# Edge counting of a graph layer moved into the attention stages, in groups of 16 nodes instead of 32

## The chip, the cores and the metric

The kernel runs on one core of a Trainium2 chip. The time is that of the device, in microseconds (us). The engines are TensorE (PE, with its weight loads as PEld), VectorE (DVE), ScalarE (ACT), GpSimd (POOL) and SyncE (SP); here SP only issues transfers. Each engine is fed by its own sequencer, which also executes register operations and branches; the trace shows those under the engine's name with a q (PEq, PEldq, DVEq).

## The reference, cut to what matters

One block of a graph transformer over N = 1250 nodes of 768 values. `_gat_layer` is run twice (4 heads of 512, then 1 head of 768).

```python
xn = layernorm(x)
# GAT layer: edges (src, dst), 41250 of them sorted by dst, and one loop per node added
h = xn @ W;  al_s, al_d = h . a_src, h . a_dst
e = leaky_relu(al_s[src] + al_d[dst], 0.2)
m = segment_max(e, dst);  ex = exp(e - m[dst])
alpha = ex / (segment_sum(ex, dst)[dst] + 1e-16)
out = segment_sum(h[src] * alpha, dst) + bias
# mix: linear attention with random features, 8 heads of 96
q, k, v = (xn @ qkv_w.T + qkv_b), q and k scaled
phi = exp(q @ rf.T - |q|^2/2);  kv = phi_k.T @ v
attn = phi_q @ kv / (phi_q @ sum(phi_k));  mix = attn @ proj_w.T + proj_b
x = x + gat2(elu(gat1(xn))) + mix
x = x + experts(layernorm(x))      # 32 experts, 2 groups x 2 experts per token
```

## The kernel before

The stages run one after another, each in its own block; at the end of a block all engines meet, and all stages keep to this order: `norm_phase`, `mix_half_phase` and `numerator` for half 0 (4 heads), the same for half 1, `proj_phase`, `logits` with `edge_table`, `count_phase`, `mask_phase`, `gat1_phase`, `gat2_project_phase`, `gat2_phase`, routing and experts. Inside a block each engine runs its own list in the order in which it is written; semaphores join them. Nodes are worked on in NT = 10 tiles of P = 125.

**The graph as counts.** The kernel never gathers along edges. It builds the dense matrix c[dst, src] of edge multiplicities and works with masks and weighted sums over it. `edge_table` loads src and dst as 324 rows of 128 edges, splits each source into a part `hi` and a rest `slo` below SLO = 314 (SPLIT = 4 parts), and forms the key dst·4 + hi. Transposed on PE they are `keyT` and `sloT`. Since dst is sorted, a group of WIN = 32 nodes touches a short span of rows; DVE and a PARTITION_ALL_REDUCE on POOL find the NW = 40 spans, in steps of RB = 4 rows.

**`count_phase`** (profile lines L779 on) works through the 40 groups, 4 heads by 10 tiles, one group beside one gemm. PE: a 12-matmul gemm for h of that head and tile (L863), a matmul that opens the PSUM sum `count_S` (L867), then a loop over the span's steps, each with 4 matmuls (L872) of a one-hot [128 edges x 128 keys] with a one-hot [128 edges x 314 sources], and one that closes the sum (L878). DVE makes both one-hots of a step (L842 one instruction, L848 four) into a ring of 4 steps ahead of PE. The bounds of the loop are read from the table at run time (value loads, L809 and L810), the branch is L814, and the ring's slot is worked out in registers. For the edges of these inputs there are 120 steps, 3 in most groups. ACT moves h and the counts out; SP stores the counts.

**`mask_phase`** loads the counts back with a node's four parts side by side, adds the loops (L974), makes the mask (ACT, L1008), finds the maxima m (DVE, L987) and transposes the count tiles (PE, L1024).

**A mix half** does one tile at a time (`tile`): transposes of q (L590), gemm q of the next tile (L580), transposes of k, gemm k, the two pairs of feature matmuls (L598), gemm v, and the 16 halves of `keys_values` (L608). DVE adds biases and norms, ACT squares, copies and takes exponentials, POOL copies the next tile of xnT into `mix_xs`. The first gemm waits for the weights and for `mix_rfT`.

**`gat2_project_phase`** goes twice through the ten tiles of h1 (q = 0 to 19). SP loads each (L1275) when the product before last is done, along with weights and masks, and at q = 12 all of x1 (`x<-x_dram`), with the residual, for the next stage.

Of the kernel before, what the change touches and what calls it, by code (L numbers as in the profile page):

```python
# [7 lines left out]
F16 = mybir.dt.float16  # L8
# [20 lines left out]
RB = 4  # L29
# [3 lines left out]
WIN = 32  # L33
NW = 40
SPLIT = 4
SLO = 314
# [85 lines left out]
def norm_phase(nc, cx, x, ident, xnT, load_next):  # L122
# [4 lines left out]
        ("stats_done", "sqrt_done", "xn_ready", "transposed", "used_dve", "used_act", "id_done"))  # L127
    dve_step = cx.sem("norm_dve_step")
    HT = NT // 2
    with ExitStack() as st:  # L130
# [7 lines left out]
        xn = [sb(nc, st, f"xn{b}", [P, D]) for b in range(2)]  # L138
        tp = [[pb(nc, st, f"tp{b}{h}", [128, 3, P]) for h in range(2)] for b in range(2)]
        block = st.enter_context(nc.Block())  # L140

        @block.sync
        def _(sp):
            for h in range(2):
                rows_dma(sp, xa[:, h * HT:(h + 1) * HT, :],
                         x.rearrange("(t p) d -> p t d", p=P)[:, h * HT:(h + 1) * HT, :], x_loaded[h])
            load_next(sp)

        @block.gpsimd
        def _(pool):  # L150
            pool.memset(ident[:], 0.0).then_inc(id_done, 1)
            pool.wait_ge(id_done, 1)
            pool.affine_select(out=ident[:], in_=ident[:], compare_op=ALU.not_equal, fill=1.0, base=0,
                               pattern=[[-1, 128]], channel_multiplier=1).then_inc(id_done, 1)

        @block.vector
        def _(dve):
            step = Chain(dve, dve_step)
            for t in range(NT):
# [12 lines left out]
            def scaled(t, b):  # L172
                dve.wait_ge(transposed, t + 1)
                dve.tensor_scalar(xn[b][:], xa[:, bass.ds(t, 1), :], mv[:, bass.ds(t, 1), 0],
                                  rstd[:, bass.ds(t, 1)], ALU.subtract, ALU.mult).then_inc(xn_ready, 1)

            def copy(t, b):
                dve.wait_ge(transposed, t + 3)
                dve.tensor_copy(xnT[:, 0:3, bass.ds(t * P, P)], tp[b][0][:]).then_inc(used_dve, 1)

            scaled(0, 0)
            with dve.Fori(0, NT // 2 - 1) as i:
                for b in range(2):
                    scaled(i * 2 + (b + 1), 1 - b)
                    copy(i * 2 + b, b)
            scaled(NT - 1, 1)
            copy(NT - 2, 0)
            copy(NT - 1, 1)

        @block.scalar  # L190
        def _(act):
            act.wait_ge(stats_done, 1)
            act.activation(std[:], veps[:], ACT.Sqrt).then_inc(sqrt_done, 1)
            with act.Fori(0, NT // 2) as i:
                for b in range(2):
                    act.wait_ge(transposed, i * 2 + (b + 3))
                    act.activation(xnT[:, 3:6, bass.ds(i * (2 * P) + b * P, P)], tp[b][1][:],
                                   ACT.Copy).then_inc(used_act, 1)

        @block.tensor  # L200
        def _(pe):
            pe.sem_inc(transposed, 2)
            pe.sem_inc(used_dve, 2)
            pe.sem_inc(used_act, 2)
            pe.wait_ge(id_done, 2)
            with pe.Fori(0, NT // 2) as i:
                for b in range(2):
                    pe.wait_ge(xn_ready, i * 2 + (b + 1))
                    pe.wait_ge(used_dve, i * 2 + (b + 1))
                    pe.wait_ge(used_act, i * 2 + (b + 1))  # L210
                    for k in range(KD):
                        last = pe.transpose(tp[b][k // 3][:, k % 3, :], xn[b][:, k * 128:(k + 1) * 128],
                                            ident[0:P, 0:P])
                    last.then_inc(transposed, 1)

# [226 lines left out]
def load_mix_weights(sp, half, wqkvT, qkv_b, w, brow, w_loaded):  # L442

    HW = D // 2
    for c in range(3):
        cols = slice(c * D + half * HW, c * D + (half + 1) * HW)
        sp.dma_start(w[:, :, c, :], wqkvT[:, cols].rearrange("(k p) n -> p k n", p=128)).then_inc(w_loaded, 16)
        sp.dma_start(brow[:, c, :], qkv_b[cols].partition_broadcast(128)).then_inc(w_loaded, 16)


def mix_half_phase(nc, cx, half, rfT_dram, xnT, ident, w, brow, w_loaded, attn, gnn_w1, a_src, a_dst, wa, load_next):


# [4 lines left out]
    SCALE = MD ** -0.5  # L458
    tag = f"mix{half}_"
    (rf_loaded, staged, q_done, k_done, v_done, q_evac, k_evac, v_evac, qsq, ksq, q_ready, k_ready, q_turned,  # L460
     k_turned, qT_done, kT_done, phi_a, phi_b, exp_a, exp_b, kv_step, kv_copied, consts) = (
        cx.sem(tag + s) for s in
        ("rf_loaded", "staged", "q_done", "k_done", "v_done", "q_evac", "k_evac", "v_evac", "qsq", "ksq", "q_ready",
         "k_ready", "q_turned", "k_turned", "qT_done", "kT_done", "phi_a", "phi_b", "exp_a", "exp_b", "kv_step",
         "kv_copied", "consts"))
# [3 lines left out]
    with ExitStack() as st:  # L469
        rfT = sb(nc, st, tag + "rfT", [A, RF])  # L470
# [1717 lines left out]
```

## Time and profile before

| what | value |
|---|---|
| median of 3 runs | 2376.53 us (2363.14 to 2378.86) |
| the profiled execution | 2375.32 us, span in the trace 2373.5 us |
| PE busy | 2108.3 us, 89% |
| DVE busy | 1124.8 us, 47% |
| ACT busy | 413.1 us, 17% |
| POOL busy | 202.7 us, 9% |

The span is what lies between the first and last record of the trace; 1.8 us lie around it. [...] Stages in the trace, by their first record: norm 0 to 42.6, mix half 0 to 212.9 with its numerator to 257.1, half 1 to 431.5 and 473, projection to 581.8, logits and edge table to 604.1, counting to 901.9, masks to 985.8, GAT 1 to 1365, then the rest.

### The profile page before, as it was taken

How to read it: one execution, taken by the hardware profiler on the slowest of the kernel's cores; microseconds unless marked ns; L12 is line 12 of the kernel's file. 1: busy time of each engine (PE TensorE's matmuls, PEld its weight loads, DVE VectorE, ACT ScalarE, POOL GpSimd, SP SyncE). 2: the span in 40 equal slices, each digit the busy share in tenths (PEclk: the TensorE clock that was granted, in tenths of full speed). 3: DMA queues.
4: the chain of work that ended last, by engine and by line, in shares of the span. 5: the costliest groups of instructions: out<-in, count | busy, mean ns of one | idle time of the engine just before them, and what ended most of it. 6: DMA issues, size and time to landing. Idle time of an engine off the chain costs nothing. (4 is left out here: it accounts for less than half of the span.)

```text
span 2373.5 us, 33698 instructions
## 1 busy us (share of the span) xinstructions
PE 2108.3 (89%) x9786; PEld 1471.1 (62%) x9787; DVE 1124.8 (47%) x2406; ACT 413.1 (17%) x743; POOL 202.7 (9%) x198
## 2 busy tenths in 40 slices
PE   4998999879799994299999979898986799999997
PEld 2666666644355553288888845454564577777776
DVE  4114211436566665788888700206636333333433
ACT  1222121200111113222222200001100122122221
POOL 0000000000000001000000000000001133323332
PEclk9999999889899995599999989998975799999999
DMA  7002200172200007633433265622125488898654
GB/s 224 0 0 70 90 0 0 43 221 71 92 25 22 24 22 246 212 96 116 121 97 98 73 220 180 168 85 75 42 59 216 123 243 258 253 285 283 187 140 78
DMA packets 79502, 288.38 MB, mean 121 GB/s; under 512 B 10780, under 2 KB 31328, under 8 KB 69837
## 3 DMA queue, kind: packets, MB, share of 16 engines
q1 hardware_dynamic: 57894, 220.18, 28.0%
q0 software_dynamic: 14688, 54.19, 9.7%
q10 hardware_dynamic: 6854, 13.15, 1.6%
q8 instruction: 40, 0.66, 0.1%
q14 instruction: 26, 0.21, 0.0%
HBM read 225.48 MB, written 62.00 MB: 121 GB/s over the span
## 5 line engine op out<-in xcount | busy, mean ns | idle before, releaser
L1215 PE MATMUL gat_Z<-h,gat_wt 125*125 125x256 f32 (+1 forms) x1600 | 355.0, 381 | 20.7 <-DVE gat_wt L1131 20.7
L1215 PEld LDWEIGHTS gat_Z<-h,gat_wt 125*125 125x125 f32 x1600 | 298.2, 188 | 66.1 <-DVE gat_wt L1131 21.2
L580 PE MATMUL mix_G<-mix_w,mix_xs 128*125 128x384 f32 x720 | 242.6, 488 | 0.0
L1363 PE MATMUL gat2p_Y<-gat2p_w,gat2p_hT 128*125 128x386 f32 (+1 forms) x640 | 211.8, 493 | 19.8 <-DMA gat2p_w<-in_L_gnn_W 10.4
L863 PE MATMUL count_G<-gnn_w,xnT 128*125 (+1 forms) x480 | 214.1, 596 | 15.3 <-issue 15.3
L2033 PE MATMUL ex_PH<-ex_xT,ex_w 128*128 128x128 f32 x1872 | 223.5, 278 | 3.0 <-issue 1.0
L2043 PE MATMUL ex_PY<-ex_w,ex_hT 128*128 128x384 f32 x624 | 215.1, 495 | 3.3 <-ACT ex_hT L1982 2.8
L2033 PEld LDWEIGHTS ex_PH<-ex_xT,ex_w 128*128 128x128 f32 x1872 | 214.3, 193 | 4.8 <-issue 4.4
L1363 PEld LDWEIGHTS gat2p_Y<-gat2p_w,gat2p_hT 128*125 128x125 f32 x640 | 121.0, 190 | 109.2 <-issue 14.2
L580 PEld LDWEIGHTS mix_G<-mix_w,mix_xs 128*125 128x125 f32 x720 | 133.1, 189 | 84.9 <-issue 2.2
L2043 PEld LDWEIGHTS ex_PY<-ex_w,ex_hT 128*128 128x128 f32 x624 | 114.3, 190 | 80.3 <-ACT ex_hT L1982 5.9
L863 PEld LDWEIGHTS count_G<-gnn_w,xnT 128*125 128x125 f32 x480 | 88.4, 189 | 114.7 <-issue 113.2
L1477 PE MATMUL gat_Z<-h,gat_wt 125*125 125x385 f32 (+1 forms) x400 | 132.4, 494 | 11.0 <-DVE gat_wt L1435 11.0
L842 DVE SCALAR_TENSOR_TENSOR count_A<-count_ikey,count_off,keyT 128x512 f32 x120 | 90.2, 751 | 96.6 <-issue 63.9
L533 DVE TENSOR_REDUCE mix_nrm<-mix_sq 125x4 f32<-125x384 f32 x40 | 22.1, 553 | 215.5 <-ACT mix_sq L553 215.5
L1477 PEld LDWEIGHTS gat_Z<-h,gat_wt 125*125 125x125 f32 x400 | 76.0, 190 | 67.4 <-DVE gat_wt L1435 11.6
L848 DVE TENSOR_SCALAR count_B<-count_islo,sloT 128x314 f16 x480 | 112.1, 298 | 0.0
L1953 DVE TENSOR_SCALAR ex_idS<-ex_ids 128x1 int32 x52 | 8.0, 154 | 214.5 <-DMA out_rows<-ex_y,ex_idS 214.5
L1923 DVE SCALAR_TENSOR_TENSOR ex_Q<-posm,offs,ex_iota 125x1280 bf16<-125x1280 f32 x55 | 85.3, 1552 | 42.7 <-issue 38.5
L1904 POOL DMA_INDIRECT out_rows<-ex_y,ex_idS x52 | 82.5, 1586 | 267.6 <-DVE ex_y L1955 223.1
L370 PE MATMUL proj_Y<-proj_w,proj_aT 128*125 128x384 f32 x240 | 83.1, 506 | 12.5 <-DVE proj_x L410 12.5
L1990 ACT ACTIVATE ex_y<-ex_PY,ex_gate 128x384 f32<-128x384 f32 x52 | 30.2, 580 | 280.6 <-DMA out_rows<-ex_y,ex_idS 242.9
(293 smaller groups left out, 2343.8 us busy)
## 6 DMA issues: line engine op xcount, KB each, us to landing
ex_w<-in_L_ffn_W SPq DMA_DIRECT2D x64, 1152.0 KB, 8.6
gat_cnt<-c_dram SPq DMA_DIRECT2D x50, 546.9 KB
gat2p_hT<-h1T_dram SPq DMA_DIRECT2D x20, 1000.0 KB, 5.0
h1T_dram<-gat_oT ACTq DMA_DIRECT2D x40, 250.0 KB, 2.0
mix_w<-in_L_mix_qkv_w SPq DMA_DIRECT2D x6, 1152.0 KB, 11.8
ct_dram<-count_out SPq DMA_DIRECT2D x40, 157.0 KB, 2.1
mix_w_slice<-in_L_gnn_W SPq DMA_DIRECT2D x6, 1024.0 KB, 11.5
proj_w2s<-in_L_gnn_W SPq DMA_DIRECT2D x4, 1536.0 KB, 26.1
```

The source lines that it names most:

```text
L370: last = pe.matmul(Y[j][:], aT[b][:, k, :], w[:, k, j * 384:(j + 1) * 384], start=(k == 0), stop=(k == KD - 1))
L580: last = pe.matmul(G[c][:], xs[b][:, k, :], w[:, k, c, :], start=(k == 0), stop=(k == KD - 1))
L842: dve.scalar_tensor_tensor(A[:, bass.ds(s * RB, RB), :], ikey[:].unsqueeze(1).to_broadcast([128, RB, 128]), off[:, bass.ds(hd * NT + t, 1) ...
L848: last = dve.tensor_scalar(B[:, bass.ds(s * RB + b, 1), :], islo[:].unsqueeze(1), sloT[:, bass.ds(r * RB + b, 1)], None, ALU.is_equal)
L863: last = pe.matmul(G[t % 2][:], xnT[:, k, t * P:(t + 1) * P], w[:, k, bass.ds(hd * C1, C1)], start=(k == 0), stop=(k == KD - 1))
L1215: last = pe.matmul(Z[b][j][:], wt[b][:, s, :], h[:, s, bass.ds(hd, 1), j * HC:(j + 1) * HC + j], start=(s == 0), stop=(s == NT - 1))
L1363: last = pe.matmul(Y[b][j][:, 0:HW if j else W], hT[q % 2][:, k, :], w[:, k, cols], start=(k == 0), stop=(k == KF - 1))
L1477: last = pe.matmul(Z[b][j][:], wt[b][:, s, :], h2[:, s, 385 * j:385 * j + CW[j]], start=(s == 0), stop=(s == NT - 1))
L1904: pool.indirect_dma_start(out, bass.IndirectOffsetOnAxis(ap=idS[:, 0:1], axis=0), y[:], None, compute_op=ALU.add).then_inc(added, 16)
L1923: dve.scalar_tensor_tensor(Q[:], posm[:, :, bass.ds(e, 1)].to_broadcast([P, NT, SLOT]), offs[:, bass.ds(at, 1)], iot[:].unsqueeze(1).to_br ...
L2033: last = pe.matmul(PH[m][:], w1[:, b, k, m * 128:(m + 1) * 128], xT[:, k, :], start=(k == 0), stop=(k == KD - 1))
L2043: last = pe.matmul(PY[j][:], hT[:, k, :], w2[:, b, k, j * 384:(j + 1) * 384], start=(k == 0), stop=(k == KM - 1))
```

## The change

- **The edge table** is made in `norm_phase`, on DVE before the statistics of x. SP loads the edges; ACT issues the loads of x, of rfT (once, kept for both halves) and of the mix weights.
- **Counting** is done in the mix halves, 40 groups in each, four a tile: one after gemm q, one after gemm k, one between the two feature pairs, one between gemm v and `keys_values`. There are now NW = 80 groups of WIN = 16 nodes, SPLIT = 8 parts of 157 sources, and steps of RB = 2 rows in a ring of 8. For these inputs they are 241 steps, 3 in most groups. The features share one PSUM bank, the counts have one. Tile loops of the norm and mix stages are written out. POOL no longer copies `mix_xs`; gemms read xnT.
- **`first_layer_phase`** takes the place of `logits`, `count_phase` and `mask_phase`: logits, then 40 gemm units for h; from unit 3 on, after every second unit the ten transposes of one count tile; after unit 30 those of m. DVE and ACT make masks beside it, now stored as BF16. The head's weights come in two buffers. A `cx.clear()` (semaphores set back) is added ahead of it.
- **The projection's weights** are loaded into the space of the mix weights.
- **`gat2_project_phase`** loads x1 in ten pieces, one each from q = 10 on.

```diff
-RB = 4
+RB = 2
-WIN = 32
-NW = 40
-SPLIT = 4
-SLO = 314
+WIN = 16
+NW = 80
+SPLIT = 8
+SLO = 157
...
 def norm_phase(...)
         @block.vector
         def _(dve):
             step = Chain(dve, dve_step)
+            dve.wait_ge(loaded, 8 * 16)
+            step(dve.tensor_copy(df[:], di[:]))
+            step(dve.tensor_copy(sf[:], si[:]))
+            step(dve.tensor_scalar(hi[:], sf[:], float(SLO), None, ALU.is_ge))
+            for part in range(2, SPLIT):
+                step(dve.scalar_tensor_tensor(hi[:], sf[:], float(part * SLO), hi[:], ALU.is_ge, ALU.add))
...
 def mix_half_phase(...)
+                    def window(i):
+                        win = half * PER * NT + i
+                        lo, hi = span(dve, win)
+                        with dve.Fori(lo, hi) as r:
+                            n = dve.snap(turn)
+                            s = dve.snap(n & (RING - 1), min_val=0, max_val=RING - 1)
+                            dve.wait_ge(used, n)
+                            dve.scalar_tensor_tensor(CA[:, bass.ds(s * RB, RB), :],
...
+                            for b in range(RB):
+                                last = dve.tensor_scalar(CB[:, bass.ds(s * RB + b, 1), :], islo[:].unsqueeze(1),
...
+                            last.then_inc(hot, 1)
+                            dve.reg_add(turn, turn, 1)
...
+                    def window(i, lo, hi):
+                        if i >= 1:
+                            pe.wait_ge(s_evac, i)
+                        pe.matmul(S[:], czero[:], islo[:], start=True, stop=False, skip_group_check=True)
+                        with pe.Fori(lo, hi) as _:
+                            n = pe.snap(count)
+                            s = pe.snap(n & (RING - 1), min_val=0, max_val=RING - 1)
+                            pe.wait_ge(hot, n)
+                            for b in range(RB):
+                                last = pe.matmul(S[:], CA[:, bass.ds(s * RB + b, 1), :].rearrange("p o k -> p (o k)"),
...
+                            last.then_inc(used, 1)
+                            pe.reg_add(count, count, 1)
+                        pe.matmul(S[:], czero[:], islo[:], start=False, stop=True, skip_group_check=True
+                                  ).then_inc(counted, 1)
...
+                    for t in range(NT):
+                        more = t + 1 < NT
+                        turn(0, t)
+                        if more:
+                            gemm(0, t + 1, q_done, q_evac)
+                        window(PER * t, *span(pe, half * PER * NT + PER * t))
+                        turn(1, t)
+                        if more:
+                            gemm(1, t + 1, k_done, k_evac)
+                        window(PER * t + 1, *span(pe, half * PER * NT + PER * t + 1))
+                        features(t, 0)
+                        window(PER * t + 2, *span(pe, half * PER * NT + PER * t + 2))
+                        features(t, 1)
+                        if more:
+                            gemm(2, t + 1, v_done, v_evac)
+                        window(PER * t + 3, *span(pe, half * PER * NT + PER * t + 3))
+                        keys_values(t, not more)
...
 def first_layer_phase(...)
+            for g in range(1, UNITS):
+                unit(g)
+                t = (g - MASK0) // 2
+                if g >= MASK0 and (g - MASK0) % 2 == 0 and t < NT:
+                    pe.wait_ge(looped, t + 1)
...
+                    for s in range(NT):
+                        last = pe.transpose(T[t % 2][s // 4][0:P, s % 4 * P:(s % 4 + 1) * P],
+                                            ct[t % 2][:, s * P:(s + 1) * P], ident[0:P, 0:P])
...
 def gat2_project_phase(...)
-                elif q - 2 == NT:
-                    rows_dma(sp, x1, x1_dram.rearrange("(t p) d -> p t d", p=P), x_loaded)
+                if q >= NT:
+                    rows_dma(sp, x1[:, q - NT, :], x1_dram[(q - NT) * P:(q - NT + 1) * P, :], x_loaded)
```

How it moves instructions. PE in a mix tile, before: transposes of k, gemm k, both feature pairs, gemm v and `keys_values` stand in one row of matmuls (the same names as in the trace; the brackets name the semaphores).

```order
L590 MATMUL mix_TQ<-ident,mix_qs 97x125 [waits mix0_qT_done,mix0_k_ready]
L590 MATMUL mix_TQ<-ident,mix_qs 97x125 x3
L580 MATMUL mix_G<-mix_w,mix_xs 125x384 [waits mix0_k_evac]
L580 MATMUL mix_G<-mix_w,mix_xs 125x384 x5
L598 MATMUL mix_PH<-mix_rfT,mix_kT 125x256 [waits mix0_exp_a,mix0_kT_done]
L598 MATMUL mix_PH<-mix_rfT,mix_kT 125x256
L598 MATMUL mix_PH<-mix_rfT,mix_kT 125x256 [waits mix0_exp_b]
L598 MATMUL mix_PH<-mix_rfT,mix_kT 125x256
```

The same place after, from the loop of the third group of a tile to the second feature pair (REGISTER_ALU, ISA and the branch are the sequencer's).

```order
L753 REGISTER_ALU [waits mix0_count_hot]
L753 ISA
L753 REGISTER_ALU
L753 MATMUL mix_count_S<-mix_count_B,mix_count_A 128x157
L753 ISA
L753 REGISTER_ALU
L753 MATMUL mix_count_S<-mix_count_B,mix_count_A 128x157
L757 ISA
L748 COMPARE_AND_BRANCH
L758 MATMUL mix_count_S<-mix_count_islo,mix_count_zero 128x157
L723 MATMUL mix_PH<-mix_rfT,mix_kT 125x256 [waits mix0_k_exped,mix0_kT_done]
L723 MATMUL mix_PH<-mix_rfT,mix_kT 125x256
```

A loop with two matmuls a step, whose wait stands on a register operation, now lies between the feature pairs, and three more like it elsewhere in the tile.

DVE at the start of the norm stage, before: the statistics come first.

```order
L163 BN_STATS stats<-xa 125x6 [waits norm_x_loaded0]
L163 BN_STATS stats<-xa 125x6 x9
L163 BN_STATS stats<-xa 125x6 [waits norm_x_loaded1]
L163 BN_STATS stats<-xa 125x6 x9
L166 BN_AGGR mv<-stats 125x2 [waits norm_dve_step]
L166 BN_AGGR mv<-stats 125x2 x9
```

And after, from the start of the table.

```order
L194 CAST edge_df<-edge_di 108x384 [waits edge_loaded]
L195 CAST edge_sf<-edge_si 108x384 [waits norm_dve_step]
L196 TENSOR_SCALAR edge_hi<-edge_sf 108x384 [waits norm_dve_step]
L198 SCALAR_TENSOR_TENSOR edge_hi<-edge_sf,edge_hi 108x384 [waits norm_dve_step] x6
L199 SCALAR_TENSOR_TENSOR edge_slo<-edge_hi,edge_sf 108x384 [waits norm_dve_step]
L200 SCALAR_TENSOR_TENSOR edge_key<-edge_df,edge_hi 108x384 [waits norm_dve_step]
L201 TENSOR_REDUCE edge_rng<-edge_df 108x3
```

The whole table, with its wait for the edges, stands ahead of the statistics of x.

## Rows read from the trace of the kernel before

**Rows 1.** The page: busy time, share and instructions of each engine.
```profile
PE 2108.3 (89%) x9786; PEld 1471.1 (62%) x9787; DVE 1124.8 (47%) x2406; ACT 413.1 (17%) x743; POOL 202.7 (9%) x198
```

**Rows 2.** Windows: us; busy PE, PEld, DVE, ACT, POOL; clock, DMA share, GB/s.
```profile
42.60:212.90 170.30, 163.59 (x684) 110.16 (x684) 31.35 (x74) 45.88 (x70) 8.57 (x12) 0.99 0.08 32
...
581.80:604.10 22.30, 17.39 (x52) 5.19 (x52) 9.91 (x32) 1.76 (x4) 1.62 (x5) 0.81 0.29 89
604.10:901.90 297.80, 283.42 (x1040) 143.05 (x1040) 190.84 (x600) 41.21 (x80) 0.98 (x6) 0.98 0.10 38
901.90:985.80 83.90, 26.87 (x110) 22.88 (x110) 62.46 (x95) 26.76 (x40) 10.90 (x21) 0.50 0.79 255
```

**Rows 3.** Timeline of PE, a mix tile: start, duration, group, [idle before].
```profile
75.25 0.59 PE L590 MATMUL mix_TQ<-ident,mix_qs 125*97 125x125 f32 x4
75.68 4.04 PE L580 MATMUL mix_G<-mix_w,mix_xs 128*125 128x384 f32 x12
...
89.46 1.92 PE L608 MATMUL mix_KV<-mix_vs,mix_phik 125*128 125x97 f32 x16
91.22 0.59 PE L590 MATMUL mix_TQ<-ident,mix_qs 125*97 125x125 f32 x4
```

**Rows 4.** Timeline of PE in counting: a gemm and what follows it.
```profile
623.70 5.31 PE L863 MATMUL count_G<-gnn_w,xnT 128*125 128x512 f32 x12
628.85 0.30 PE L867 MATMUL count_S<-count_islo,count_zero 128*128 128x314 f16 x1
```

**Rows 5.** PE's sequencer by line: duration ns, first and last start (us).
```profile
L809 PEldq TENSOR_LOAD <-spans x1: 313/313/313, 621.7 to 621.7; - x1
L814 PEldq MOVE  x1: 29/29/29, 623.1 to 623.1; - x1
L815 PEldq MOVE  x3: 29/29/29, 742.8 to 745.9; - x3
L872 PEldq FUSED_REGOPS  x4: 74/74/79, 743.0 to 743.7; - x4
L632 PEldq COMPARE_BRANCH  x1: 207/207/207, 88.9 to 88.9; - x1
```

**Rows 6.** Timeline of DVE: start of the norm stage, start of the edge table.
```profile
12.15 4.70 DVE L163 BATCH_NORM_STATS2 stats<-xa 125x6 f32<-125x384 f32 x10 [12.02 <-DMA xa<-in_x]
...
591.87 0.36 DVE L733 CAST edge_df<-edge_di 108x384 f32<-108x384 int32 x1 [10.33 <-DMA edge_si<-in_src]
...
593.06 1.15 DVE L737 SCALAR_TENSOR_TENSOR edge_hi<-edge_sf,edge_hi 108x384 f32<-108x384 f32 x2
```

**Rows 7.** Timeline of PE and POOL: first gemm of mix 0, start of counting.
```profile
47.36 12.10 PE L580 MATMUL mix_G<-mix_w,mix_xs 128*125 128x384 f32 x36
...
612.46 0.24 POOL L830 IOTA count_ikey<- 128x128 f32 x1 [11.17 <-issue]
...
615.16 6.82 PE L863 MATMUL count_G<-gnn_w,xnT 128*125 128x512 f32 x12 [15.31 <-issue]
```

**Rows 8.** Timeline of DVE in counting: two steps, then the next group's first.
```profile
617.09 0.75 DVE L842 SCALAR_TENSOR_TENSOR count_A<-count_ikey,count_off,keyT 128x512 f32 x1
...
618.65 0.75 DVE L842 SCALAR_TENSOR_TENSOR count_A<-count_ikey,count_off,keyT 128x512 f32 x1
...
621.43 0.75 DVE L842 SCALAR_TENSOR_TENSOR count_A<-count_ikey,count_off,keyT 128x512 f32 x1 [1.17 <-issue]
```

**Rows 9.** Timeline of PE: matmuls after gaps of some 2 us, and without.
```profile
205.53 0.67 PE L590 MATMUL mix_TQ<-ident,mix_qs 125*97 125x125 f32 x4 [1.97 <-DVE mix_qs L534]
...
213.48 10.36 PE L247 MATMUL mix_F<-mix_qT,mix_rfT 97*128 x24 [1.90 <-ACTq L264]
...
420.11 1.15 PE L590 MATMUL mix_TQ<-ident,mix_qs 125*97 125x125 f32 x4 [1.97 <-DVE mix_qs L534]
...
454.20 8.59 PE L247 MATMUL mix_F<-mix_qT,mix_rfT 97*128 x24
```

**Rows 10.** Timeline of PE in `gat2_project_phase`.
```profile
1529.18 33.00 PE L1363 MATMUL gat2p_Y<-gat2p_w,gat2p_hT 128*125 128x384 f32 x96 [9.42 <-DMA gat2p_hT<-h1T_dram]
```

More of the change, by code:

```diff
@@ L181, in _, with scaled @@
[L181 to L188, printed above, removed]
+            def scaled(t):
+                if t >= 2:
+                    dve.wait_ge(transposed, t - 1)
+                dve.tensor_scalar(xn[t % 2][:], xa[:, t, :], mv[:, t, 0:1], rstd[:, t:t + 1], ALU.subtract, ALU.mult
+                                  ).then_inc(xn_ready, 1)
@@ L200, in _ @@
         @block.tensor
         def _(pe):
-            pe.sem_inc(transposed, 2)
-            pe.sem_inc(used_dve, 2)
-            pe.sem_inc(used_act, 2)
             pe.wait_ge(id_done, 2)
[L206 to L214, printed above, removed]
+            pe.wait_ge(key_ready, 1)
@@ L475, in mix_half_phase @@
         with ExitStack() as st1:
-            xs = [sb(nc, st1, tag + f"xs{b}", [128, KD, P]) for b in range(2)]
             qs = sb(nc, st1, tag + "qs", [P, 2, HH, A])
@@ L574, in gemm @@
-                def gemm(c, t, b, done, evac):
-                    if c == 0:
-                        pe.wait_ge(staged, t + 1)
-                    if evac is not None:
+                pe.sem_inc(used, RING)
+                def gemm(c, t, done, evac):
+                    if t == 0:
+                        pe.wait_ge(w_loaded[c], 16 * (half + 1))
+                    else:
                         pe.wait_ge(evac, t)
                     for k in range(KD):
-                        last = pe.matmul(G[c][:], xs[b][:, k, :], w[:, k, c, :], start=(k == 0), stop=(k == KD - 1))
+                        last = pe.matmul(G[c][:], xnT[:, k, t * P:(t + 1) * P], w[:, k, c, :], start=(k == 0),
+                                         stop=(k == KD - 1))
@@ L976, in _ @@
             loop(0)
+            loop(1)
+            dve.wait_ge(al_turned, 1)
+            step(dve.tensor_copy(al[:], T[1][0][0:P, 0:NT * J].rearrange("p (t j) -> p t j", j=J)))
             dve.wait_ge(rows_loaded, 64)
@@ L1026, in _, with unit @@
-            pe.wait_ge(copied, NT)
-            pe.wait_ge(m_ready, 1)
-            for j in range(3):
-                for t in range(width[j]):
-                    last = pe.transpose(T[0][j][0:H1, t, :], m[:, 4 * j + t, :], ident[0:P, 0:P])
-                last.then_inc(m_turned, 1)
+            def unit(g):
+                hd, t = g // NT, g % NT
+                if t == 0:
+                    pe.wait_ge(w_loaded[hd % 2], 16 * (hd // 2 + 1))
+                if g >= 2:
+                    pe.wait_ge(h_evac, g - 1)
+                for k in range(KD):
+                    last = pe.matmul(G[g % 2][:], xnT[:, k, t * P:(t + 1) * P], w[hd % 2][:, k, :],
+                                     start=(k == 0), stop=(k == KD - 1))
+                last.then_inc(gemm, 1)
@@ new lines, in _ @@
+            for c in range(CH):
+                for k in range(KD):
+                    last = pe.matmul(T[0][c][0:J, 0:CHW[c]], wa[:, k, :], xnT[:, k, CHO[c]:CHO[c] + CHW[c]],
+                                     start=(k == 0), stop=(k == KD - 1))
+                last.then_inc(rows_done, 1)
+            unit(0)
+            pe.wait_ge(rows_copied, CH)
+            for t in range(NT):
+                last = pe.transpose(T[1][0][0:P, t * J:(t + 1) * J], alT[:, t * P:(t + 1) * P], ident[0:J, 0:J])
```

720 lines of the change are left out of this document (320 added, 400 removed).

## The prediction

> **What bounds the kernel now.** I read the page's busy shares first: PE is busy 89% of the span, DVE 47%, and nothing else comes near [rows 1]. So the question for every stage is whether PE is packed there, and I read the stages one by one in the view of windows [rows 2]. In the mix half PE is busy 163.59 of 170.30 us, in counting 283.42 of 297.80. The stage after counting is different: in the 83.9 us of the mask stage PE works 26.87 us at a granted clock of 0.50, DVE 62.46. Then the timeline of PE, for what a packed stage consists of. A mix tile runs from 75.25 to 91.22, 15.96 us, with no idle time in its rows: a transposition group of 0.43, a 12-matmul gemm of 3.9, and 1.8 for KV [rows 3]. A group of counting begins with one gemm of 5.15 us (623.70 to 628.85), and its count matmuls follow without a gap [rows 4]. Last the sequencer's own records, which the page does not count as busy [rows 5]: they are what the moved work is made of.
>
> **What goes.** From the end of the projection stage to the start of the first GAT block, 581.80 to 985.80 (its last 0.1 included), the kernel spends 404.1 us. After the change one block stands there: logits and their transposes (16.7 of the 17.39 us in [rows 2]; six edge transposes leave), 40 gemm units of 5.15 = 206.0, 100 count transposes and 10 of m. In the mask stage 110 transposes took 26.87 us at half clock, 0.24 each; at full clock, between gemms, I take half, so 13.2. With 0.9 for the last evacuation, 1.4 for the end of the block and 1.0 for the clearing that is added: 239.2. That is **−165**. DVE's 62.5 us and ACT's 26.8 of mask work lie beside it: a mask tile has two units and ten transposes, 11.5 us, for 6.2 of DVE, so they cost nothing; were one mask tile late each time, the stage would be bound by DVE at 62, still under the gemms. Bounds: −155 (transposes at half clock) to −170.
>
> **Edge table in the norm stage.** DVE begins its statistics at 12.15, after waiting for x [rows 6]. Now it first does the table. In its own stage DVE was busy 9.91 us [rows 2], almost all with the table; about 1.2 of it comes after the reduction. Four more comparisons (1.15 for two, [rows 6]) and tables twice as wide bring the rest to 11.7. The edges landed 9.3 us into the old block (581.8 plus a wait that ends at 591.87, [rows 6]), and now share the queues with x, so DVE starts on them at 9 to 15, ends at 21 to 27, and then has 9.4 of statistics (4.70 a half) that before began at 12.15 and could run only as x came in; they end 5 to 12 later; the tail (final operations on the spans, two copies) adds 2.2. Together **+10**, from +5 to +14.
>
> **Starts of the mix halves.** After PARTITION_ALL_REDUCE POOL's next operation came 11.17 us later with nothing waited for but "issue", and PE's first gemm of counting stood at 615.16, 11.1 us into its block; in mix half 0 it stood at 47.36, 4.8 in [rows 7]. The change puts the reduction and then IOTA in that order around the start of mix half 0, whose gemm now waits for the constants. Between 0 and +6.3; the row with the same order of operations is the nearest, so **+5.5**. Half 1 has no reduction before it and no load of rfT: **−1**. The last stores of counts at each end: **+1**.
>
> **Counting in the mix tiles.** It costs PE little and its sequencer much. The array: count matmuls of 157 columns cost about what KV's of 97 do, 0.11 (1.8 for 16, [rows 3]), so a window with 6 of them and its two borders is 0.8, four in a tile 3.2. The sequencer: two loads of a span and what follows take 1.4 (621.7 to 623.1); an iteration took 1.56 for 4 matmuls (three starts between 742.8 and 745.9); and one matmul's register work 0.245 (four between 743.0 and 743.7) [rows 5]. With 2 matmuls an iteration is then 1.56 − 0.49 = 1.07, and a window of three steps 1.4 + 3.2 = 4.6. Before, 1.4 + 3 × 1.56 = 6.1 of this in a group lay beside 7.1 of array work (283.42 / 40). Now, for 15.96 + 3.2 us of array work, there are 4 × 4.6 = 18.4 of sequencer work, and what decides is how far the sequencer may be ahead. It executed the tile's loop branch at 88.9, when KV, which stands ahead of that branch, began at 89.46 [rows 3, 5]: it was some 17 matmuls ahead and no further. So a window is hidden only behind what directly precedes it:
> - KV, turn 0 and gemm q run 6.1 us on the array; window 0 is hidden and adds 0.7;
> - turn 1 and gemm k (4.3) stand beside issuing them and window 1's 4.6 of sequencer work: 4.7 until its end;
> - window 2 has only two feature matmuls ahead: 4.7, almost all of it idle array;
> - the second features and gemm v (4.7) hide window 3, which adds 0.8: 5.5.
>
> The period is 21.7, with 0.2 for semaphores 21.9: **+5.9 a tile**. The first tile of a half has +5.5, eight have 47.2, and the last, where windows follow one another with no gemm between, +11.3. A half is +64 and both **+128**. Bounds: 3.2 a tile (all hidden), which makes +80, and 18.4 a tile beyond the array (nothing hidden), which is excluded by the first bullet.
>
> **DVE in the tile.** An iteration took it 1.56 (617.09 to 618.65) and a new span 1.17 more [rows 8]. Its work halves, to 0.8; its register work does not quite. I take 1.1, as on PE: 4 × (1.17 + 3.3) + 2.9 of its other work = 20.8, under 21.9, so it costs nothing, but only just. ACT's copies of the counts (four of 0.4) are beside.
>
> **The clock.** Window 2 leaves the array nearly idle for 3.4 us in each tile. Gaps of 1.9 to 2.0 us were followed by half clock in two places: the transposes at 420.11 took 1.15 where those at 205.53, after an equal gap, took 0.67; and the 24 matmuls after a gap of 1.90 at 213.48 took 10.36 against 8.59 without one at 454.20 [rows 9]. So a gap costs 0 to 1.8. I take 1.45 for 18 tiles and 2 for the ends: **+28**, bounds 0 and 36.
>
> **gat2_project.** PE waits 9.42 us at 1529.18 for hT [rows 10], whose load stands on SP's queue behind the one load of all of x (3.84 MB). In ten pieces, each issued after an hT, it holds none up. **−11**, with 1.6 for slower matmuls after the gap, an estimate by the pair at 213.48 and 454.20 [rows 9]; what is next late is nothing I see, since the weights' and masks' loads stay where they are. At least −5.
>
> **Sum.** +10 + 5.5 − 1 + 1 + 128 + 28 − 165 − 11 = −4.5. The profiled execution took 2375.3 (span 2373.5), 1.2 under the median of 2376.5. So 2370.8, rounded to **2370**: a large gain behind and nearly as large a loss ahead of it. About 1% (24 us) is what a measurement of this kernel can tell from no change.
>
> [...]
>
> **Rivals.**
> - **A, the clock holds.** The sparse matmuls of window 2 count as work, as after the gap at 205.53. 2370 − 28 = 2342. For: 205.53; against: 213.48 and 420.11.
> - **B, the sequencer's work is hidden.** Then a tile is 15.96 + 3.2 = 19.2, a half 9 × 3.2 + 11 = 40 instead of 64, and nothing lets the clock fall: 2370 − 48 − 28 = 2294. Against: the lead of 17 matmuls, and that windows 1 to 3 need 4.6 each with 0.8, 4.3 and 4.7 beside them.
> - **C, slower: DVE sets the tile.** PE's step waits for DVE's count masks in its sequencer, so everything behind it waits, the next gemm too. The point is (21.9 − 2.9)/4 − 1.17 over 3 = 1.19 us an iteration. At 1.4 the period is 24.4, +2.5 × 20 = +50: 2420; at the old 1.56 it is 26.4, 2460. For: DVE's reads of registers, its wait and its branch do not shrink with the tile; against: half its array work goes.
>
> **Chances.** The forecast 0.40, A 0.25, B 0.11, C 0.24. The range takes in A with the bounds of the small terms, and C up to 1.4 us an iteration: 2325 to 2418; B and the far end of C stay out. Faster by over 1% are A and B: 0.36; slower by over 1% is C: 0.24; the rest 0.40.
>
> **What would show it.** In the new profile: tiles of the mix halves of 21 to 23 us, with PE idle under "issue" in the third window and granted clock under 1 behind it; a first-layer block of about 239 with PE packed; the norm stage some 10 longer; POOL's IOTA late in mix half 0; no wait of PE for hT in gat2_project. I would be wrong by a period of 19 or of 25, and PE's waits in its sequencer for DVE's steps would show the latter.

## The result, and the profile after

The changed kernel takes **2417.2 us** (median of 4, 2414.9 to 2419.3); the kernel before took 2369.8 in the runs beside it (4, 2361.1 to 2378.9). The ratio is 1.020, interval 1.015 to 1.025: **slower by 2%**, where 2370 was forecast. The time is at the top of the range (2325 to 2418), the direction is that of rival C. The kernel before has times in two groups, 2361 to 2363 and 2376.5 to 2379 here, for which the last section has a likely stage; its profiled execution is of the upper one. The profiled executions took 2375.3 and 2416.7 us; their traces span 2373.5 and 2414.9 from the first record to the last, 1.8 less each, and differ by 41.4. I account for those.

By stage, from the first record of one to that of the next:

| stage | before | after | change | forecast |
|---|---|---|---|---|
| norm | 42.6 | 68.4 | +25.8 | +10 |
| mix half 0 | 170.4 | 276.0 | +105.6 | +83 |
| mix half 1 | 174.4 | 261.2 | +86.8 | +78 |
| first layer (logits, counting, masks before) | 404.1 | 236.0 | −168 | −165 |
| gat2_project | 231.0 | 219.3 | −11.7 | −11 |
| all others | 1351 | 1354 | +3 | 0 |

So what the change took away went as forecast, and what it added cost 16 more in the norm stage and 31 more in the mix halves. The page and the windows of the changed kernel, to be held against [rows 1, 2] (columns as there; norm, mix half 0, mix half 1, first layer):

```profile
PE 2150.9 (89%) x9868; PEld 1479.2 (61%) x9869; DVE 1132.5 (47%) x2533; ACT 405.9 (17%) x773; POOL 189.5 (8%) x182
```
```profile
0.00:68.40 68.40, 11.32 (x66) 8.82 (x67) 34.79 (x93) 6.36 (x13) 2.52 (x11) 1.00 0.47 123
68.40:344.45 276.05, 236.25 (x1006) 149.23 (x1006) 130.27 (x437) 45.53 (x101) 1.33 (x6) 0.86 0.09 31
386.00:647.20 261.20, 231.86 (x1004) 147.20 (x1004) 128.80 (x433) 44.24 (x100) 1.69 (x6) 0.88 0.10 33
...
801.00:1036.90 235.90, 234.19 (x636) 106.22 (x636) 63.17 (x96) 51.04 (x83) 11.07 (x22) 0.99 0.33 104
```

The first-layer stage has PE busy 234.2 of 235.9 at a clock of 0.99, as forecast. In the mix halves two things show at once: PE is no longer packed, and its clock is 0.86 and 0.88, where mix half 0 had 0.99 [rows 2].

The timeline of PE in one mix tile of the changed kernel, which answers to [rows 3]:

```profile
141.60 0.63 PE L715 MATMUL mix_TQ<-ident,mix_qs 125*97 125x125 f32 x4
142.06 4.04 PE L704 MATMUL mix_G<-mix_w,xnT 128*125 128x384 f32 x12
145.94 0.23 PE L747 MATMUL mix_count_S<-mix_count_islo,mix_count_zero 128*128 128x157 f16 x1
...
147.21 0.48 PE L753 MATMUL mix_count_S<-mix_count_B,mix_count_A 128*128 x2 [0.63 <-DVE mix_count_B L630]
...
147.85 0.64 PE L715 MATMUL mix_TQ<-ident,mix_qs 125*97 125x125 f32 x4
148.33 4.04 PE L704 MATMUL mix_G<-mix_w,xnT 128*125 128x384 f32 x12
152.20 0.23 PE L747 MATMUL mix_count_S<-mix_count_islo,mix_count_zero 128*128 128x157 f16 x1
...
152.76 1.07 PE L723 MATMUL mix_PH<-mix_rfT,mix_kT 97*125 97x256 f32 x4
153.89 0.24 PE L747 MATMUL mix_count_S<-mix_count_islo,mix_count_zero 128*128 128x157 f16 x1
154.45 0.48 PE L753 MATMUL mix_count_S<-mix_count_B,mix_count_A 128*128 x2 [0.32 <-issue]
155.51 0.52 PE L753 MATMUL mix_count_S<-mix_count_B,mix_count_A 128*128 x2 [0.58 <-DVE mix_count_B L630]
156.61 0.54 PE L753 MATMUL mix_count_S<-mix_count_B,mix_count_A 128*128 x2 [0.58 <-DVE mix_count_B L630]
...
157.25 2.04 PE L723 MATMUL mix_PH<-mix_rfT,mix_kT 97*125 97x256 f32 x4
159.09 6.14 PE L704 MATMUL mix_G<-mix_w,xnT 128*125 128x384 f32 x12
165.06 0.23 PE L747 MATMUL mix_count_S<-mix_count_islo,mix_count_zero 128*128 128x157 f16 x1
...
167.42 0.63 PE L715 MATMUL mix_TQ<-ident,mix_qs 125*97 125x125 f32 x4
```

This tile takes 25.8 us (141.60 to 167.42). The mean of 16, the first period of each half left out, is 25.3, the shortest 24.3, for 15.96 before; with those two (22.8 and 21.7) it is 24.9. Windows 1 and 3 cost their 0.6. Window 2 lasts 3.3, as forecast. Not as forecast: window 0 lasts 1.9 (145.94 to 147.85), and PE there waits for DVE; and behind window 2 the features and gemm v take 1.8 + 6.0 us, where in the kernel before they took 0.9 + 3.9 at a clock of 1.00 (two pairs of features from 83.86 to 85.59, gemm v to 89.46). The granted clock of that stretch is 0.61:

```profile
157.25:165.00 7.75, 7.75 (x17) 4.61 (x17) 3.42 (x11) 0.90 (x2) 0.00 (x0) 0.61 0.03 10
```

In nine of the 16 tiles that pair takes 6.3 to 6.5, in the others 7.4 to 7.9, 7.0 on the mean.

In window 2 the view puts two gaps down to DVE. PE's own sequencer records (154.04, 155.10 and 156.19, where its three steps begin, 1.1 apart) follow each other with nothing between that looks like a wait: the sequencer is busy all through the window, and DVE has finished each step 0.02 to 0.1 us before PE's sequencer comes to it. PE's busy time holds none of this: from 153.9 to 157.2 it is 1.74 us of 3.30, that of 8 matmul records. In window 0 it is otherwise: the sequencer stands from 143.1 to 144.6, until DVE's first step is done.

### The profile page after: what moved, and what is told of

Read it like the earlier page. It is cut to its first block and busy times, and to the rows that moved or that the text cites. A ratio compares the mean times of both kernels' runs of the same rounds, so it can differ in the third digit from the quotient of the medians.

```text
span 2414.9 us, 34923 instructions
## 1 busy us (share of the span) xinstructions
PE 2150.9 (89%) x9868; PEld 1479.2 (61%) x9869; DVE 1132.5 (47%) x2533; ACT 405.9 (17%) x773; POOL 189.5 (8%) x182
## 5 line engine op out<-in xcount | busy, mean ns | idle before, releaser
L704 PE MATMUL mix_G<-mix_w,xnT 128*125 128x384 f32 x720 | 267.1, 526 | 8.9 <-POOL mix_count_zero L602 8.9
L704 PEld LDWEIGHTS mix_G<-mix_w,xnT 128*125 128x125 f32 x720 | 146.8, 208 | 109.0 <-issue 33.9
L947 PE MATMUL first_G<-gnn_w,xnT 128*125 128x512 f32 x480 | 208.3, 593 | 0.0
L624 DVE SCALAR_TENSOR_TENSOR mix_count_A<-mix_count_ikey,mix_count_off,keyT 128x256 f32 x241 | 116.8, 485 | 159.4 <-issue 80.2
L947 PEld LDWEIGHTS first_G<-gnn_w,xnT 128*125 128x125 f32 x480 | 89.1, 188 | 110.3 <-issue 110.3
L753 PE MATMUL mix_count_S<-mix_count_B,mix_count_A 128*128 x482 | 75.9, 238 | 50.2 <-DVE mix_count_B L630 28.3
L630 DVE TENSOR_SCALAR mix_count_B<-mix_count_islo,sloT 128x157 f16 x482 | 103.3, 259 | 0.1
L753 PEld LDWEIGHTS mix_count_S<-mix_count_B,mix_count_A 128*128 x482 | 41.1, 98 | 90.5 <-issue 85.7
L444 PE MATMUL proj_Y<-mix_w,proj_aT 128*125 128x384 f32 x240 | 83.0, 505 | 13.7 <-DVE proj_x L484 13.7
```

Of the source, the lines that this page charges most:

```text
L444: last = pe.matmul(Y[j][:], aT[b][:, k, :], w[:, k, j * 384:(j + 1) * 384], start=(k == 0), stop=(k == KD - 1))
L624: dve.scalar_tensor_tensor(CA[:, bass.ds(s * RB, RB), :], ikey[:].unsqueeze(1).to_broadcast([128, RB, 128]), off[:, win:win + 1], keyT[:, ...
L630: last = dve.tensor_scalar(CB[:, bass.ds(s * RB + b, 1), :], islo[:].unsqueeze(1), sloT[:, bass.ds(r * RB + b, 1)], None, ALU.is_equal)
L704: last = pe.matmul(G[c][:], xnT[:, k, t * P:(t + 1) * P], w[:, k, c, :], start=(k == 0), stop=(k == KD - 1))
L753: last = pe.matmul(S[:], CA[:, bass.ds(s * RB + b, 1), :].rearrange("p o k -> p (o k)"), CB[:, bass.ds(s * RB + b, 1), :].rearrange("p o k ...
L947: last = pe.matmul(G[g % 2][:], xnT[:, k, t * P:(t + 1) * P], w[hd % 2][:, k, :], start=(k == 0), stop=(k == KD - 1))
```

## Experiments on the mix tile

**Early squares.** DVE's timeline of the same tile says where window 0's wait is from:

```profile
140.74 0.55 DVE L646 TENSOR_REDUCE mix_nrm<-mix_sq 125x4 f32<-125x384 f32 x1 [3.84 <-ACT mix_sq L676]
...
143.74 0.48 DVE L624 SCALAR_TENSOR_TENSOR mix_count_A<-mix_count_ikey,mix_count_off,keyT 128x256 f32 x1 [1.58 <-issue]
...
144.85 0.49 DVE L624 SCALAR_TENSOR_TENSOR mix_count_A<-mix_count_ikey,mix_count_off,keyT 128x256 f32 x1 [0.28 <-issue]
```

and ACT's, at the end of that tile:

```profile
165.82 0.30 ACT L669 ACTIVATE mix_count_out<-mix_count_S 128x157 f32<-128x157 f32 x1 [5.90 <-PE mix_count_S L758]
166.02 0.93 ACT L676 ACTIVATE mix_sq<-mix_qs 125x384 f32<-125x384 f32 x2
```

ACT's squares of the next tile stand behind its copy of window 3's sum, so they come after PE's last window; DVE's norms wait for them, its windows for the norms. I moved them up; `squares(t)` holds the lines taken out below.

```diff
+                squares(0)
                 for t in range(NT):
-                    for c, (evac, squared, ready) in enumerate(((q_evac, qsq, q_ready), (k_evac, ksq, k_ready))):
-                        act.wait_ge(evac, t + 1)
...
-                        act.activation(sq[:, c, :, :], qs[:, c, :, 0:MD], ACT.Square).then_inc(squared, 1)
...
                     act.activation(phik[:, 2:4, :], PH[:], ACT.Exp).then_inc(exped, 1)
+                    if t + 1 < NT:
+                        squares(t + 1)
                     keep_counts(PER * t + 3)
```

> The changed kernel with one order on ScalarE altered: the squares of the next tile stand ahead of the copy of the tile's fourth count sum, not behind it. Theory (PE waits in window 0 because DVE's first step comes late, DVE because the norms wait for squares that ACT makes only after the fourth window): window 0 takes 0.6 us, as window 1 does, not 1.9; a tile of 23.5 us for 24.9; the kernel at 2392, 25 us under the changed one. Rival (DVE's own pace of 1.1 us a step and 1.5 a new span is the limit): the wait only moves to another window, 2412 to 2420.

Measured: 2365.0 (10 runs), 0.997 of before (0.995 to 1.000), 52 us under the changed kernel; the tile fell to 22.5, of which six in sixteen take 21.3 to 21.6 and the rest some 23. One that takes 21.3, PE, from window 0:

```profile
145.62 0.23 PE L752 MATMUL mix_count_S<-mix_count_islo,mix_count_zero 128*128 128x157 f16 x1
...
146.18 0.61 PE L720 MATMUL mix_TQ<-ident,mix_qs 125*97 125x125 f32 x4
...
152.05 0.24 PE L752 MATMUL mix_count_S<-mix_count_islo,mix_count_zero 128*128 128x157 f16 x1
...
155.41 1.10 PE L728 MATMUL mix_PH<-mix_rfT,mix_kT 97*125 97x256 f32 x4
156.35 4.04 PE L709 MATMUL mix_G<-mix_w,xnT 128*125 128x384 f32 x12
```

Window 0 takes 0.6, as the theory said, and the gain is double what it said: with that first gap gone the clock also holds behind window 2 in more than a third of the tiles (1.00 from 155.41 to 160.3 in this one, for 0.61 above; why in those is open). The theory on window 0 holds; it priced half of what the edit gave.

**Fill.** Is it the idle array that brings the clock down?

```diff
                             last.then_inc(used, 1)
+                            if i % PER == 2:
+                                for b in range(2):
+                                    pe.matmul(S[:], zero[:], xnT[0:P, 0, 0:SLO], start=False, stop=False, ...)
```

> The changed kernel with two more matmuls of a zero weight (f32, 157 columns, some 0.2 us each) behind each step of window 2, so that the array works where it stood idle under issue. They add zero to the sum. Theory (the idle array in window 2 is what brings the clock down for the second features and gemm v): these two run at full clock, 4.8 us for 6.6 together, -1.7 to -2.3 a tile, against up to 0.2 us a step for the added work: 2385 to 2395. Rival (their slowness has another cause, weights or reads in conflict): 2417 to 2430.

Measured: 2368.0 (10 runs), 49 under the changed kernel, a tile of 23.3. PE behind window 2:

```profile
155.75 1.06 PE L723 MATMUL mix_PH<-mix_rfT,mix_kT 97*125 97x256 f32 x4
156.65 4.04 PE L704 MATMUL mix_G<-mix_w,xnT 128*125 128x384 f32 x12
```

The granted clock of mix half 0 rose from 0.86 to 0.94. PE is given more to do, 60 matmuls in that half (120 records in the trace: 1126 for 1006), and the kernel becomes faster: the pair behind window 2 takes 4.8 us at a clock of 1.00 here (155.75 to 160.52), for 7.8 at 0.61, so its slowness was the clock alone. The ten times stand in two groups, 2365 to 2368 and 2379 to 2382. The last section shows a stage from which such a step of 12 can come; against the upper group, to which the profiled execution (2378.0 of span) belongs, the gain is 37, or 2.0 for each of 18 tiles.

**Static spans.** Without register work on both engines, and on PE alone:

```diff
-                        with pe.Fori(lo, hi) as _:
-                            n = pe.snap(count)
-                            s = pe.snap(n & (RING - 1), min_val=0, max_val=RING - 1)
+                        lo, hi = SPANS[win]
+                        first = 1 + sum(h - l for l, h in SPANS[half * PER * NT:win])
+                        for n in range(first, first + hi - lo):
+                            s = n & (RING - 1)
                             pe.wait_ge(hot, n)
```

> The changed kernel with the spans of these inputs written into the program, on PE and on DVE, so that neither loads bounds, branches or works out slots at run time; the instructions on the arrays are the same ones. It gives up that the kernel works for any edge list. Theory (the sequencers' work is the price of the move): a tile falls from 24.9 to between 19.2 and 19.6, 15.96 plus 0.8 for each window, the clock holds behind window 2, and the kernel comes to 2297 (2285 to 2310). Rival (count matmuls, PSUM sharing or ACT's extra copies set the tile): 2390 or more.

> As the one with static spans, but on PE alone; DVE still loads bounds and branches. It gives up that PE works for any edge list. Theory (both sequencers are near the limit, and DVE's chain of windows behind the norms is next): DVE's 4 x (1.5 + 3.2) + 4 of other work and waits give a tile of 23 us, the kernel 2376. Rival A (PE's sequencer alone is the price): 19.5 a tile, 2300. Rival B (DVE alone is): no change, 2412 to 2420.

Measured: on both engines 2288.9 (4 runs), 0.965 of before (0.961 to 0.969); on PE alone 2377.8 (10 runs), 1.003 (1.001 to 1.006), with a tile of 22.9. With both static a tile takes 18.8, and window 2 costs what its matmuls do, 0.95 us to the next features (125.14 to 126.09) with 0.22 of wait for ACT:

```profile
125.14 0.23 PE L750 MATMUL mix_count_S<-mix_count_islo,mix_count_zero 128*128 128x157 f16 x1
125.22 0.58 PE L756 MATMUL mix_count_S<-mix_count_B,mix_count_A 128*128 128x157 bf16 x6
125.64 0.23 PE L759 MATMUL mix_count_S<-mix_count_islo,mix_count_zero 128*128 128x157 f16 x1
126.09 1.10 PE L724 MATMUL mix_PH<-mix_rfT,mix_kT 97*125 97x256 f32 x4 [0.22 <-ACT mix_phik L689]
```

With PE alone static, PE waits for DVE's steps in window 2 instead:

```profile
150.61 0.31 PE L756 MATMUL mix_count_S<-mix_count_B,mix_count_A 128*128 128x157 bf16 x2 [0.96 <-DVE mix_count_B L631]
151.73 0.31 PE L756 MATMUL mix_count_S<-mix_count_B,mix_count_A 128*128 128x157 bf16 x2 [0.80 <-DVE mix_count_B L631]
```

Both came within 9 us of what was expected. The same matmuls and masks cost 128 us less once no sequencer has to find out where they are: that is the price of run-time bounds in windows as small as these, with what they do to the clock (0.95 in mix half 0 with both static, 0.86 in the changed kernel). It is owed on both engines, each nearly as slow as the other (PE 1.10 a step, DVE 1.08): with PE's register work gone, window 2 still lasts 3.25 in most tiles, for 3.4, now by DVE alone, and 39 of the 128 us are won. DVE alone made static was not run; that PE would keep the window as long rests on its sequencer's records above.

**Groups of 32.** If the number of windows and steps is what costs, the old sizes should be better in the new place: NW = 40, WIN = 32, SPLIT = 4, RB = 4, a ring of 4, and two windows a tile.

```diff
                         window(PER * t, *span(pe, half * PER * NT + PER * t))
                         turn(1, t)
                         if more:
                             gemm(1, t + 1, k_done, k_evac)
-                        window(PER * t + 1, ...)
                         features(t, 0)
-                        window(PER * t + 2, ...)
                         features(t, 1)
                         if more:
                             gemm(2, t + 1, v_done, v_evac)
-                        window(PER * t + 3, ...)
+                        window(PER * t + 1, ...)
```

> The changed kernel with the sizes of before for counting: 40 groups of 32 nodes by 314 sources in steps of 4 rows, a ring of 4 steps; so two windows in a tile, one behind gemm q and one behind gemm v. Theory (what costs is the number of windows and steps, 4 x 4.6 us of sequencer work a tile, now 2 x 6.1, each behind a gemm): a tile of 19.8, 15.96 plus 1.9 for each window, no fall of the clock, and two tiles' ends 8 us shorter each: 2306 (2295 to 2325). Rival (DVE is late for the first window in this order of ACT, as with 16 nodes): 21.5 to 23 a tile, 2340 to 2365.

Measured: 2382.1 (10 runs), 1.006 of before (1.003 to 1.008): this was off by 76 us. A tile takes 23.9 on the mean, since PE waits for DVE in window 0, which lasts 4.2 us for 1.9:

```profile
144.49 1.07 PE L749 MATMUL mix_count_S<-mix_count_B,mix_count_A 128*128 x4 [0.53 <-DVE mix_count_B L630]
146.06 1.16 PE L749 MATMUL mix_count_S<-mix_count_B,mix_count_A 128*128 x4 [0.51 <-DVE mix_count_B L630]
```

That was the rival, which named ACT's order, at a price still higher than it had. So the same kernel with the squares early:

> The kernel with 40 groups of 32 nodes, and ACT's squares of the next tile ahead of its last copy of counts. Theory (with 32 nodes the first window still took 4.3 us for 1.9, because DVE started it only after norms that wait for that copy; its second and third step came late): the tile falls from 23.9 to 20.7 (19.9 and 0.8 for the features that now wait for each other), the kernel from 2382 to 2315. Rival (DVE cannot make three steps of 1.56 behind a new span of 1.5 in time in any order): 22.5 a tile or more, 2350 to 2375.

Measured: 2329.5 (4 runs), 0.982 of before (0.977 to 0.987). The tile is 20.8, as expected, 15.96 and 3.9 of windows and 0.8 of waits between the feature pairs, which now have nothing between them; the total is 14 above what I expected. The tile's 3.1 less, 16 or 18 times, make the 53 us that were won; my 67 were more than that sum, and had no term for the rest.

```profile
145.64 1.03 PE L724 MATMUL mix_PH<-mix_rfT,mix_kT 97*125 97x256 f32 x4
147.45 1.10 PE L724 MATMUL mix_PH<-mix_rfT,mix_kT 97*125 97x256 f32 x4 [0.78 <-ACT mix_phik L688]
```

## Experiments on the norm stage, x1, and all together

In the changed kernel the edge table starts at 29.9, not at 9 to 15 as I had it, and the statistics after it. DVE, and POOL with PE where mix half 0 begins (the forecast's [rows 6, 7]):

```profile
29.92 0.36 DVE L194 CAST edge_df<-edge_di 108x384 f32<-108x384 int32 x1 [29.79 <-DMA edge_si<-in_src]
...
41.41 9.29 DVE L223 BATCH_NORM_STATS2 stats<-xa 125x6 f32<-125x384 f32 x20
```
```profile
79.95 0.24 POOL L599 IOTA mix_count_ikey<- 128x128 f32 x1 [10.98 <-issue]
```
```profile
80.85 13.81 PE L704 MATMUL mix_G<-mix_w,xnT 128*125 128x384 f32 x36 [8.87 <-POOL mix_count_zero L602]
```

**Weights late:** ACT issues rfT and the mix weights only after the edges.

```diff
+            act.wait_ge(loaded, 8 * 16)
             act.dma_start(rfT[0:MD, :], rf_dram).then_inc(rf_loaded, 16)
             load_next(act)
```

> The changed kernel, with ACT waiting for the edges to have landed before it issues the loads of rfT and of the mix weights (4 MB) in the norm stage. Theory (the edges landed at 29.8 us because they shared the queues with the weights as well as with x): the edges land with x at 13 to 16, DVE starts there, and the norm stage ends at 54 for 68.4; the weights land by 30, in time. The kernel at 2402. Rival (x alone or the edges' own small packets make them late): DVE starts at 25 or later, 2412 to 2418.

Measured: 2407.9 (4 runs), 9 less where 15 were expected. The table starts at 23.1, the next block at 62.0 for 68.4, 6.4 earlier: less than half of the expected 14. The weights held the edges up by 7 us, and by what x or the edges' own loads hold them up beyond 15 was not tried apart.

**Statistics first**, the edge table behind them on DVE:

```diff
+            for t in range(NT):
+                if t % HT == 0:
+                    dve.wait_ge(x_loaded[t // HT], 32)
+                for h in range(2):
+                    last = dve.bn_stats(stats[:, t, h, :], xa[:, t, h * 384:(h + 1) * 384])
...
             dve.wait_ge(loaded, 8 * 16)
             step(dve.tensor_copy(df[:], di[:]))
```

> The changed kernel with DVE doing the statistics of x ahead of the edge table. Theory (9.3 us of statistics stand behind a wait for edges although x is there earlier): they run between 14 and 30, the table from 30 to 41.5, and the stage ends at 59 for 68.4: 2408. Rival (x is as late as the edges): no change, 2415 to 2419.

Measured: 2411.0 (2401.3 to 2414.4, 4 runs), 6 less where 9 were expected; the stage ended at 58.3, 10.1 earlier, as expected to within a microsecond.

**IOTA early:** one more IOTA behind the reduction.

```diff
             pool.partition_all_reduce(allb[:], best[:], EGP, ...).then_inc(span_max, 1)
+            pool.iota(again[:], [[WIN, NW]], base=0, channel_multiplier=0, ...)
```

> The changed kernel with one more IOTA on POOL, into a buffer nobody reads, right behind PARTITION_ALL_REDUCE in the norm stage. Theory (going from the reduction to IOTA costs POOL 11 us once, whenever it comes): they pass beside DVE's statistics, and the first gemm of mix half 0 comes 4.8 us into its block for 12.4: the kernel 7.6 us shorter, 2409.6. Rival (the 11 us belong to the start of a block or to mix half 0's own constants): the first gemm stays at 12 us, 2415 to 2419.

Measured: 2404.8 (4 runs), 12 less for the expected 7.6. POOL's wait moved to where nobody needs it,

```profile
49.83 0.20 POOL L190 IOTA edge_again<- 108x80 f32 x1 [7.50 <-issue]
...
69.25 0.24 POOL L602 IOTA mix_count_ikey<- 128x128 f32 x1
```

and the first gemm came 2.8 us into its block, 9.6 earlier. The cost belongs to the first IOTA after a reduction: in the changed kernel two MEMSETs ran at 68.4 to 69.0 and only the IOTA behind them came late, and in half 1, with no reduction before it, the IOTA came at once (386.98). What POOL does in these 7.5 to 11 us no run shows.

**x1 alone** in the kernel before:

```diff
-                elif q - 2 == NT:
-                    rows_dma(sp, x1, x1_dram.rearrange("(t p) d -> p t d", p=P), x_loaded)
+                if q >= NT:
+                    rows_dma(sp, x1[:, q - NT, :], x1_dram[(q - NT) * P:(q - NT + 1) * P, :], x_loaded)
```

> The kernel before with one part of the change alone: x1 loaded in ten pieces in gat2_project. Theory (PE's wait of 9.4 us for hT goes, as it did in the changed kernel's trace): the stage 11 us shorter, 2361 against 2372. Rival (the gain needs the BF16 masks too, which halve what that queue moves): the wait stays in part, 2366 to 2372.

Measured: 2352.5 (8 runs), 0.991 of before (0.989 to 0.994), 21 us by that ratio for 11. The wait is gone and the stage 12 shorter (231 to 219), without the BF16 masks. The rest of the gain lies in the routing stage, whose code is the same; whether the edit brought it is open (last section).

**All repairs**, with groups of 16 and of 32:

> The changed kernel with 16 nodes a group and four repairs: squares early (-52 alone), statistics ahead of the edge table (-10 of the norm stage), weights after the edges (-6), IOTA early (-9). Theory (the first has its own stage; of the norm repairs the table then runs from 28.3 to 40, so that they give 13 together): 2365 - 13 - 9 = 2343. Rival (they overlap, since each takes away a wait that hides the others): 2355 to 2365.

> As the one with all repairs, with 40 groups of 32 nodes. Theory: 22 under groups of 32 with early squares, 2293 if those come to 2315; about 3% under the kernel before, and within 10 of the kernel with static spans. Rival (as there): 2330 to 2353.

Measured: 2342.3 (0.988, 0.983 to 0.993) and **2303.4** (0.971, 0.966 to 0.976; 4 runs each). The norm repairs with IOTA give nearly what was expected, with both sizes (23 and 26 us for 22). The second kernel is faster than both that were compared, by 2.9% against the one before. Its norm stage is 52.1. Its mix halves, 52.6 and 45.5 us longer than before where the changed kernel's are 105.6 and 86.8 longer, have PE busy for 94% of their time, at clock 0.97 and 0.99:

```profile
52.10:275.00 222.90, 209.84 (x964) 137.66 (x964) 125.40 (x374) 42.10 (x81) 1.73 (x6) 0.97 0.10 39
318.60:538.50 219.90, 207.00 (x964) 135.84 (x964) 125.07 (x373) 40.80 (x80) 1.78 (x6) 0.99 0.10 39
```

## Why the prediction was wrong, step by step

- **What goes: right.** −168 for −165, PE packed and the masks hidden; gat2_project −11.7 for −11.
- **Counting, the bullet on window 0: wrong.** "Window 0 is hidden and adds 0.7": it took 1.9, 1.2 more in each tile. I reckoned DVE's pace (1.1 a step taken, 1.08 measured), found that it "costs nothing", and did not ask when it may start. Its first step stands behind norms, squares and ACT's copy of the window before, which closes a ring through all three engines once a tile. The experiment on the squares undid this: 52 us with what it did to the clock, enough for the changed kernel to draw level.
- **The other windows: right in mechanism.** Window 2 took 3.3 to 3.5 (2.3 where it has two steps), with PE's sequencer busy throughout; window 1, with turn 1 and gemm k, 4.9 for 4.7. What the forecast did not see is that DVE alone would keep window 2 at 3.25 (171.39 to 174.64 with PE alone static), so that relief on one engine buys little: 39 of 128 us. Its lead of "17 matmuls" held: at 141.62 the sequencer loaded window 0's bounds with 16 records ahead of them (4 transposes and gemm q's 12) just beginning. Those are records of the trace, not matmuls of the program: a gemm's 6 matmuls have 12 there (360 for the 180 of mix half 0), KV's 8 have 16, a transpose of q has one. Apart from the clock a tile was 23.0 for 21.9, and window 0's 1.2 more is that difference.
- **The clock: right in mechanism, mis-sized.** 1.6 to 3.2 a tile and not 1.45, 2.2 on the mean (7.0 for 4.8), some 40 us in 18 tiles for 26. The filled window shows it is the clock (0.94 for 0.86 in mix half 0). That the loose stretch in window 0 adds to it is what the early squares suggest: there the pair takes 5.9 on the mean. The 31 us of the mix halves are these two: 1.2 and 0.8 more in each of 16 tiles.
- **Norm stage, wrong by 16:** "DVE starts on them at 9 to 15" was 29.9. I took the edges' landing from a stage with less to load (2.0 MB, 8.4 here), where by its row it came 10.1 us into the block, not 9.3, and bounded their wait by x alone. The mix weights held them up by 7 us; the rest of the 15 is open. The statistics, behind the table by my own count, carried the delay to the end of the stage; moved ahead of it they gave back 10 us.
- **The start of mix half 0:** +7.7 for +5.5, above my bound of 6.3; half 1 −1.9 for −1. The mechanism, POOL's IOTA after the reduction, is shown by the early IOTA.
- **Rivals.** A is refuted, B too: only static programs come to B's price, by taking the work away, not by hiding it. C named the right engine and the wrong price: DVE was not too slow, it began too late; that the tile came to the 25 us named as its sign is luck. Together the misses are 16 + 31 − 3 − 1 + 3 = 46, the distance from −4.5 to +41.4.

## What to carry to other kernels

Before moving a loop with run-time bounds beside other work, count the sequencer's time of a window (here 1.4 to load the bounds and 1.1 a step on PE, 1.2 to 1.6 and 1.1 on DVE) and put the window only behind a packed stretch that is longer; few large windows beat many small ones here (2329.5 against 2365.0, both with the squares early). Then follow, for each engine that feeds it, not its pace but the order in which its program lets it begin: one copy in front of the next tile's first step closed a ring worth 52 us. A load that is fast in one stage must be priced again among the loads of the stage that it moves to.

## What the runs showed of the hardware that I had not expected

**A stage whose clock can go either way.** The kernel before has times of 2353 to 2381 in the runs beside these, and the kernel with x1 alone 21 us of gain for a stage 12 us shorter. The traces of the two show one further difference, in the routing stage, whose code is the same. Kernel before:

```profile
1750.85:1794.40 43.55, 36.96 (x180) 36.84 (x180) 15.70 (x46) 6.33 (x12) 0.74 (x1) 0.50 0.48 153
```

with x1 alone:

```profile
1736.90:1767.80 30.90, 21.42 (x180) 20.99 (x180) 14.98 (x46) 6.34 (x12) 0.74 (x1) 0.87 0.61 183
```

The same 180 matmul records took 36.96 us in a stage at a clock of 0.50, or 21.42 at 0.87; the first stage of routing 43.8 us or 30.9, and the one behind it about 58 in both. In the second the clock rose soon after its matmuls began (the first group of transposes takes 2.73 in both, the gemm behind it 2.58 or 1.73) and held to the last of them. All other traces of the study have the form at 0.50 (median of one gemm record 0.40 us in each of them, 0.28 with x1 alone). The clock over a whole run goes with its time: of 24 runs of the kernel before in one series, the nine of 2359 to 2367 us have 0.932 to 0.935, the fifteen of 2370 to 2381 have 0.924 to 0.930. The eight runs with x1 alone all have 0.932 or more, so the edit may favour the faster form; the changed kernel, with the same edit, has 0.925 to 0.927 in all four. What decides it was not tried; but some 12.5 us can come or go with it, more than several of the effects above, so that only the lengths of the stages themselves settle those.

**Adding matmuls made the kernel faster**: 116 with a zero weight (232 records in the trace, 10100 for 9868), in place of idle time, bought 37 to 49 us.
